# One attention and mixture-of-experts layer on one core: the four engines' work lists written out again in smaller pieces

## The chip, the cores and the metric

The kernel runs on one core of a Trainium2 chip. The metric is the device time of one execution in microseconds. In the text, PE is TensorE (matrix products and transposes), DVE is VectorE, ACT is ScalarE, POOL is GpSimd, and SP is SyncE, which only issues transfers. Every engine works through its own list of instructions in order; an instruction starts when the semaphores that stand before it in the list have reached their values.

## The reference

Input `x` has 4 batches of 512 tokens of 128 features. There are two halves, each with a residual:

```python
x = x + _layernorm(_L0_attn_ref(_layernorm(x), w_qkv, w_out))
x = x + _layernorm(_L0_ffn_ref(_layernorm(x), router_w, w1, w2, shared_gate_up, shared_down, shared_gate_w))
# attention: 16 heads of 8 features. The tokens are permuted in rows of a snake, cut in 4 segments of 128;
# each query of a segment attends to every second key of its segment (64 keys):
scores = jnp.einsum('bhsqd,bhskd->bhsqk', qh * scale, kd)
attn = jax.nn.softmax(scores, axis=-1)
# feed forward: 8 experts, the best 2 of each token with their softmax weights, and a shared expert
routed = jnp.einsum('ne,ned->nd', combine, einsum(silu(xf @ w1[e]), w2[e]))
shared = sigmoid(xf @ shared_gate_w) * (silu(gate) * up @ shared_down)
```

All values are float32. Every expert is computed for every token and weighted, with zero where it was not chosen.

## The kernel before

**Data.** A batch is 4 tiles of 128 tokens. All weights lie in SBUF. Products that need full precision are made of a high and a low part: `q_high`/`q_low` and `k_high`/`k_low` split the projections, `w1h`/`w1l` (made by ACT and by `w_low` on POOL, L268) the expert weights, `XH`/`XL` the feed-forward input.

**Attention of a batch b**, by the names of the steps:
- `normalise_x` (ACT), `x_T` (PE transposes), `x_copy` (ACT), `qkv` (PE; it becomes `q_project` and `k_project`), `qk_high` (ACT) and `qk_low` (DVE).
- `select_k` and `select_q` (PE) spread the features so that 16 heads lie in 4 groups; `k_rows` and `q_rows` (ACT, one group on DVE) copy them out. `k_blocks` (DVE, L1185, four instructions of 96x1024) writes the block-diagonal keys `Kb`, of which there are two buffers, by the parity of the batch.
- `scores_q(b, s)` (PE, L463) makes the scores of segment s with queries on the rows, in two halves of 8 heads, into two PSUM banks; `maxima` (DVE, L1208) takes the negated maximum of each half; `max_split` splits it in two parts, `max_T` (PE, L472) transposes them, `max_rows` (ACT and DVE) copies them under the queries `Qs`. They are so subtracted within the next product.
- `scores_k(b, s)` (PE, L486) makes the scores again with keys on the rows, in two halves; `exps` (ACT, L897); `attend` (PE, L503) multiplies by values and by ones; `attended` (ACT) copies, `attend_T` (PE, L516) transposes, `divide` (DVE, L1224 and L1226) normalises two segments at a time; `output_T` (PE, L522), `o_copy` (ACT), `project` (PE, L536), `y_copy` (ACT).
- `residual`, `residual2` (DVE) take the statistics of the projected rows, add the input, and take the statistics again. `powers` (POOL, L299) raises variances to -1/2; `neg_mean` (DVE, L1165) follows. `normalise_3` (ACT), `moe_in` (PE) and `x3_high`, `x3_low` bring the result in as the feed-forward input.

**Feed forward of a batch.** `router` (PE) gives the logits; `route` and `route2` (DVE) make the softmax, the two largest, and the weights `CW`, with the exponentials on ACT (batches 0 and 1) or POOL (`router_exp`, L284). `gate`, `up`, `expert_h` (PE, L355 to L357) are the first products, `shared_o`, `expert_o` (PE, L681) the second; `tanh`, `silu`, `silu_0`, `gated` the nonlinearity; `accumulate` (DVE) and `weight` (ACT) add the weighted outputs, `add_weighted` (POOL) sums those of ACT, `finish` and `finish_out` end a batch.

**Order.** It is written out by hand in each engine's block. A prologue does batch 0 up to its scores. A loop over i = 0, 1, 2 has scores and maxima of batch i + 1 beside exponentials and attention of batch i. Then a list without a loop has the attention of the last batch beside the experts of batch 0; this list ends at `gate(1)`. A last loop has the experts of batches 1 to 3. In the loop of DVE the order around a batch's end is `maxima(i + 1, 3)`, `max_split(i + 1)`, `k_blocks(i + 2)`, `divide(i, 1)`, `max_rows(i + 1)`. The dependent steps of `route2` on DVE are joined by `link`, which adds one to a common semaphore `step` and waits for it at once. Short `warm_up` products on PE fill waits of the prologue.

## Time and profile before

| | us |
|---|---|
| three runs | 180.89, 180.92, 183.22 |
| median | 180.92 |
| the profiled execution | 180.77 |
| its span, first to last instruction | 178.9 |

Busy in the span: PE 152.5, PE's weight loads 128.9 (beside its products), DVE 132.2, ACT 113.4, POOL 46.7. The mean granted clock of TensorE is 0.958 of full speed. The page's list of the chain that ended last puts 62% of the span to PE and 26% to DVE. The transfers are small: 6.01 MB, nearly all of it in the first 14 us.

A row of the timeline has start, duration, engine, line, operation, output and inputs, count, and in brackets the idle time of the engine before it with what ended it. A row of windows has the stretch, its length, busy time and count for PE, PE's weight loads, DVE, ACT and POOL, then the granted clock as a share of full speed, the share of the DMA engines, and GB/s.

### The profile page before, as it was taken

To read this page: it belongs to the slowest core of one execution; us is meant where nothing else is said; L and a number is where in the kernel's file an instruction comes from. 1 tells how busy PE (TensorE), PEld (TensorE's weight loads), DVE (VectorE), ACT (ScalarE), POOL (GpSimd) and SP (SyncE) were. 2 spreads that over 40 slices of the span, in tenths; PEclk is the share of its full clock that TensorE was granted. 3 is DMA by queue.
4 is the path that set the end of the run, shared out by engine and by line. 5 is a ranking of instruction groups with operands and counts; after the bars stand their busy time and mean duration, and the time that the engine had idled before them with its cause. 6 is when DMAs were issued, how large, how long until landed. Compare 5 with 4: busy or idle time off the path is not lost.

```text
span 178.9 us, 3632 instructions
## 1 busy us (share of the span) xinstructions
PE 152.5 (85%) x1188; PEld 128.9 (72%) x1188; DVE 132.2 (74%) x499; ACT 113.4 (63%) x269; POOL 46.7 (26%) x47
## 2 busy tenths in 40 slices
PE   6999797895499964999789999999999899969920
PEld 5787666673298642999578887979997899869920
DVE  7579889028955999328968876958999945896793
ACT  3787683834977565555496679944689376746803
POOL 5511003202001260002200220259552098202211
PEclk9999999889999999579999999999999999999995
DMA  5990630000000000000000000000000100100101
GB/s 170 314 330 12 146 94 2 4 0 0 0 0 4 0 4 0 0 0 0 5 2 0 4 0 4 0 0 2 4 0 2 59 4 0 57 4 0 52 11 59
DMA packets 10626, 6.01 MB, mean 34 GB/s; under 512 B 753, under 2 KB 10609, under 8 KB 10609
## 3 DMA queue, kind: packets, MB, share of 16 engines
q1 hardware_dynamic: 10192, 5.58, 11.1%
q10 hardware_dynamic: 416, 0.21, 0.4%
q8 instruction: 10, 0.16, 0.4%
q14 instruction: 8, 0.06, 0.1%
HBM read 3.69 MB, written 1.05 MB: 26 GB/s over the span
## 4 chain that ended last, share of the span: by engine, by line
PE 62%; DVE 26%; ACT 4%; issue 4%; POOL 1%; POOLq 0%; ACTq 0%; DVEq 0%
PE bank L681 15%; PE bank L486 7%; DVE negm L1208 6%; PE bank L355 5%; PE bank L356 4%; PE bank L357 4%; PE bank L352 4%; PE bank L463 3%; DVE Kb L1185 3%; PE bank L503 3%; PE bank L536 2%; DVE ST L1116 2%; DVE X L1364 2%; DVE Kb L1157 1%; PE bank L411 1%
## 5 line engine op out<-in xcount | busy, mean ns | idle before, releaser
L299 POOL TENSOR_TENSOR RS<-VE,nhalf 128x4 f32<-128x4 f32 x14 | 14.1, 1009 | 90.1 <-DVE VE L1124 90.1
L1208 DVE TENSOR_REDUCE negm<-bank 128x8 f32<-128x512 f32 x32 | 20.6, 684 | 13.9 <-PE bank L463 13.8
L1364 DVE SCALAR_TENSOR_TENSOR X<-bank,CW,X 128x128 f32<-128x128 f32 x80 | 22.5, 342 | 7.8 <-PE bank L681 7.7
L681 PEld LDWEIGHTS bank<-w2n,Pr 128*128 128x128 f32 x192 | 25.0, 191 | 2.0
L897 ACT ACTIVATE Pr<-bank 128x512 f32<-128x512 f32 x32 | 18.0, 598 | 12.4 <-PE bank L486 12.1
L681 PE MATMUL bank<-w2n,Pr 128*128 128x128 f32 x192 | 25.2, 275 | 0.0
L1019 ACT ACTIVATE Pr<-bank 128x512 f32<-128x512 f32 x27 | 16.3, 604 | 11.9 <-PE bank L357 11.8
L486 PE MATMUL bank<-Qs,Kb 128*128 128x128 f32 x128 | 19.7, 296 | 0.4 <-ACT Qs L837 0.2
L486 PEld LDWEIGHTS bank<-Qs,Kb 128*128 128x128 f32 x128 | 17.8, 208 | 2.0 <-issue 0.9
L355 PE MATMUL bank<-XH,w1h 128*128 128x512 f32 x32 | 15.2, 474 | 0.0
L315 POOL TENSOR_TENSOR Tm<-Tm 128x512 f32<-128x512 f32 x7 | 9.0, 1285 | 20.2 <-ACT Tm L1034 20.2
L1034 ACT ACTIVATE Tm<-bank,CW 128x128 f32<-128x128 f32 x44 | 12.5, 369 | 2.6 <-PE bank L681 2.6
L463 PE MATMUL bank<-Kb,Qs 96*128 96x256 f32 x64 | 13.2, 326 | 0.9 <-ACT Qs L863 0.5
L356 PE MATMUL bank<-XH,w1l 128*128 128x512 f32 x32 | 12.6, 394 | 0.0
L357 PE MATMUL bank<-XL,w1h 128*128 128x512 f32 x32 | 12.6, 393 | 0.0
L463 PEld LDWEIGHTS bank<-Kb,Qs 96*128 96x128 f32 x64 | 9.6, 206 | 4.1 <-issue 2.5
L284 POOL TENSOR_TENSOR EX<-base,DL 128x36 f32<-128x36 f32 x2 | 12.3, 6132 | 0.9 <-DVE DL L1257 0.9
L503 PE MATMUL bank<-Pr,Vb 128*32 128x128 f32 x256 | 10.7, 288 | 0.0
L352 PE MATMUL bank<-Y 128*128 128x256 f32 x24 | 8.9, 514 | 1.4 <-DVE Y L1288 1.4
L516 PE MATMUL bank<-cst,AVs 128*128 128x128 f32 x32 | 6.6, 287 | 3.2 <-DVE O L1226 1.6
L889 ACT ACTIVATE AVs<-bank 128x256 f32<-128x256 f32 x16 | 6.3, 395 | 4.4 <-PE bank L503 4.4
L681 PE MATMUL bank<-w2n,hs 128*128 128x128 f32 x64 | 8.7, 279 | 0.0
(158 smaller groups left out, 351.8 us busy)
## 6 DMA issues: line engine op xcount, KB each, us to landing
X<-in_L_attn_x SPq DMA_DIRECT2D x4, 256.0 KB, 4.0
Kb<-kone SPq DMA_DIRECT2D x8, 128.0 KB, 2.7
XP<-in_x_snake SPq DMA_DIRECT2D x3, 256.0 KB, 4.0
out<-XN SPq DMA_DIRECT2D x3, 256.0 KB, 2.2
w1n<-in_L_ffn_w SPq DMA_DIRECT2D x1, 512.0 KB, 4.8
w2n<-in_L_ffn_w SPq DMA_DIRECT2D x1, 512.0 KB, 5.9
out<-XN SPq DMA_DIRECT2D x2, 128.0 KB, 1.8
wqkv_n<-in_L_attn_w_qkv SPq DMA_DIRECT2D x1, 192.0 KB, 3.4
```

The lines of the kernel that those rows point to most:

```text
L352: mm(to[:, 0:width], Y[:, 0], Y[:].rearrange("p t d -> p (t d)")[:, 0:width], start=True, stop=True)
L355: mm(out_, wh, vh, start=True, stop=False)
L356: mm(out_, wl, vh, start=False, stop=False)
L357: return mm(out_, wh, vl, start=False, stop=True)
L463: i = mm(S1[n % 2][:, j * 256:(j + 1) * 256], Qs[0:MROW, b % 2, g, s * P:(s + 1) * P], Kb[0:MROW, b % 2, g, s], start=True, stop=True)
L486: i = mm(S2[s2_bank(n)][:, j * P:(j + 1) * P], Kb[:, b % 2, g, s, 2 * pr:2 * pr + 2], Qs[:, b % 2, g, s * P:(s + 1) * P], start=True, stop ...
L503: i = mm(PC[j * VW:(j + 1) * VW, (s % 2) * 2 * P + half * P:(s % 2) * 2 * P + (half + 1) * P], Vb[:, b % 2, s, half * 4 + j], Pr[:, n % 4, ...
L681: i = mm(ps[output_bank(n, s)][:, s * P:(s + 1) * P], lhs[:, s * P:(s + 1) * P], w, start=True, stop=True)
L897: A(Pr[:, n % 4], bank(S2[s2_bank(n)], 4), ACT.Exp).then_inc(S["ex"], 1)
L1019: A((hs0 if b == 0 else hs)[:, k % 3 if k >= 0 else 3], ps[hidden_bank(n)][:], ACT.Silu).then_inc(S["sh"], 1)
L1208: V.tensor_reduce(negm[:, b % 2, s, 8 * half:8 * half + 8], bank(S1[n % 2], 8, KEYS), AX.X, ALU.max, negate=True).then_inc(S["mx"], 1)
L1364: V.scalar_tensor_tensor(out=acc[:, b, t], in0=ps[output_bank(n)][:, t * P:(t + 1) * P], scalar=CW[:, b, t, k:k + 1], in1=acc[:, b, t], op ...
```

## The change

- The loops up to `gate(1)` are gone. Each engine's list up to there is written out step by step, in a new order, with the steps of attention, router and experts mixed more finely.
- `scores_q`, `scores_k`, `maxima`, `exps` and ACT's `max_rows` are called for one half at a time in many places; `normalise_x` and `normalise_3` for single tiles. `qkv`, `qk_high`, `qk_low`, `residual` and `residual2` are cut in their parts (`q_project`, `k_project`, `q_high`, `k_high`, `q_low`, `k_low`, `spread_y`, `gather`, `add_rows`, `spread_r`). `select_k` can be called by halves.
- `link` and its semaphore `step` are gone. `route` and `route2` are cut in ten steps; two of them have a new semaphore (`iv`, `eqs`), and the sum counts on `sm`, which is now waited for at 2 per batch.
- The waits of PE for the weights of the experts stand at their first use. ACT fills the ones for the keys (`key_ones`) before its first normalisation. The two preparations of low parts on POOL stand elsewhere in its list.
- The last loop, batches 1 to 3, keeps its order; only the parts have their new names.

The core of the diff. The list of ACT, the lists of PE after batch 1 and of DVE after `max_split(2)` are left out; they alternate in the same manner.

```diff
@@ gpsimd
-            powers_0(0)
-            powers_0(1)
-            powers(0, 1)
-            key_columns(0)
-            key_columns(1)
-            powers(0, 2)
-            w_low(rwl[:], rwn[:], rwh[:], S["rwhs"], 1, S["rwls"])
-            w_low(gul[:], gun[:], guh[:], S["guhs"], 1, S["guls"])
...
+            powers_0(0)
+            powers_0(1)
+            powers(0, 1)
+            powers(0, 2)
+            powers(0, 3)
+            key_columns(0)
+            key_columns(1)
+            key_columns(2)
+            powers(1, 0)
+            experts_low()
+            powers(2, 0)
+            router_low()
+            key_columns(3)
+            powers(1, 1)
+            shared_low()
+            powers(2, 1)
+            powers(1, 2)
+            powers(2, 2)
+            add_weighted(0)
+            router_exp(2)
+            powers(1, 3)
+            powers(3, 0)
+            powers(2, 3)
+            add_weighted(1)
+            powers(3, 1)
+            router_exp(3)
+            add_weighted(2)
+            powers(3, 2)
+            add_weighted(3)
...
@@ tensor, from the end of batch 0's scores to those of batch 2
+            select_q(1, 3)
+            x_T(2)
+            max_T(0)
+            values(1)
+            k_project(2)
+            scores_k(0, 0)
+            q_project(2)
+            scores_q(1, 0, (0,))
+            scores_k(0, 1, (0,))
+            scores_q(1, 0, (1,))
+            scores_k(0, 1, (1,))
+            attend(0, 0)
+            scores_k(0, 2, (0,))
+            scores_q(1, 1)
+            attend(0, 1)
+            scores_k(0, 2, (1,))
+            scores_q(1, 2, (0,))
+            scores_k(0, 3, (0,))
+            scores_q(1, 2, (1,))
+            attend_T(0, 0)
+            attend_T(0, 1)
+            attend(0, 2)
+            scores_q(1, 3, (0,))
+            scores_k(0, 3, (1,))
+            scores_q(1, 3, (1,))
+            select_k(2, (0,))
+            attend(0, 3)
+            attend_T(0, 2)
+            select_k(2, (1,))
+            attend_T(0, 3)
+            max_T(1)
+            select_q(2, 0)
+            select_q(2, 1)
+            output_T(0)
+            select_q(2, 2)
+            select_q(2, 3)
+            scores_k(1, 0)
+            project(0)
+            scores_q(2, 0, (0,))
...
@@ scalar, start
+            key_ones()
+            normalise_x_0(0)
+            x_copy_0(0)
+            normalise_x_0(1)
+            k_high_0(0)
+            q_high_0(0)
...
@@ vector, steps of the router
-            def route2(b):
...
-                link(V.tensor_reduce(nmx[:, b, 1], EX[:, b, :, 0:E], AX.X, ALU.add))
-                dve.wait_ge(S["sm"], b + 1)
+                V.tensor_reduce(nmx[:, b, 1], EX[:, b, :, 0:E], AX.X, ALU.add).then_inc(S["sm"], 1)
...
+            def router_inverse(b):
+
+                dve.wait_ge(S["sm"], 2 * (b + 1))
                 V.reciprocal(SG[:, b], EZ[:, b]).then_inc(S["sg"], 1)
-                link(V.reciprocal(nmx[:, b, 2], nmx[:, b, 1]))
+                V.reciprocal(nmx[:, b, 2], nmx[:, b, 1]).then_inc(S["iv"], 1)
...
@@ vector, from the end of batch 0's maxima
+            maxima(0, 3)
+            max_split(0)
+            q_rows(1)
+            k_blocks(1, (1,))
+            max_rows(0)
+            k_blocks(1, (2, 3))
+            maxima(1, 0, (0,))
+            neg_mean(0, 3)
+            k_low(2)
+            maxima(1, 0, (1,))
+            q_low(2)
+            maxima(1, 1)
+            maxima(1, 2)
+            divide(0, 0)
+            maxima(1, 3)
+            max_split(1)
+            divide(0, 1)
+            k_blocks(2, (0,))
+            max_rows(1)
+            k_blocks(2, (1, 2, 3))
+            q_rows(2)
+            maxima(2, 0, (0,))
+            spread_y(0)
+            gather(1, 0)
+            maxima(2, 0, (1,))
+            maxima(2, 1, (0,))
+            neg_mean(1, 0)
+            maxima(2, 1, (1,))
+            add_rows(0)
+            maxima(2, 2, (0,))
+            spread_r(0)
+            maxima(2, 2, (1,))
+            k_low(3)
+            maxima(2, 3, (0,))
+            q_low(3)
+            maxima(2, 3, (1,))
+            divide(1, 0)
+            gather(2, 0)
+            max_split(2)
...
```

## Rows read from the trace of the kernel before

**Rows 1.** The page: busy time by engine, and the granted clock in 40 slices.
```profile
PE 152.5 (85%) x1188; PEld 128.9 (72%) x1188; DVE 132.2 (74%) x499; ACT 113.4 (63%) x269; POOL 46.7 (26%) x47
...
PEclk9999999889999999579999999999999999999995
```

**Rows 2.** Windows cut at the four `max_T` and at `gate(1)`; columns as told above.
```profile
0.00:22.67 22.67, 19.60 (x109) 15.92 (x109) 16.83 (x50) 14.94 (x34) 6.50 (x18) 1.00 0.69 194
22.67:45.74 23.07, 19.03 (x160) 13.91 (x159) 14.10 (x41) 13.63 (x31) 3.54 (x5) 0.93 0.07 17
45.74:67.43 21.69, 17.13 (x169) 13.79 (x169) 17.31 (x47) 15.59 (x34) 4.96 (x4) 1.00 0.01 2
67.43:90.55 23.12, 19.00 (x166) 16.25 (x167) 16.07 (x50) 12.13 (x26) 2.02 (x2) 0.85 0.01 1
90.55:119.37 28.82, 28.24 (x250) 24.25 (x251) 21.31 (x102) 22.55 (x55) 4.57 (x4) 1.00 0.01 1
119.37:178.90 59.53, 49.51 (x341) 44.74 (x339) 46.53 (x214) 34.59 (x93) 25.17 (x14) 0.96 0.06 19
```

**Rows 3.** Timeline of PE: the first matmul and six waits.
```profile
1.45 5.46 PE L352 MATMUL bank<-Y 128*128 128x256 f32 x12 [1.45 <-DVE Y L1288]
...
20.82 0.33 PE L424 MATMUL bank<-kch,sel 128*96 128x256 f32 x1 [0.90 <-DVE kcl L1177]
...
31.74 1.39 PE L405 MATMUL bank<-cst,XN 128*128 128x128 f32 x4 [0.97 <-ACT XN L822]
...
41.53 0.33 PE L424 MATMUL bank<-kch,sel 128*96 128x256 f32 x1 [0.88 <-DVE kcl L1177]
...
49.05 0.66 PE L522 MATMUL bank<-cst,O 128*128 128x128 f32 x4 [2.26 <-DVE O L1226]
...
63.31 0.33 PE L424 MATMUL bank<-kch,sel 128*96 128x256 f32 x1 [1.04 <-DVE kcl L1177]
...
70.81 0.66 PE L522 MATMUL bank<-cst,O 128*128 128x128 f32 x4 [2.26 <-DVE O L1226]
```

**Rows 4.** Timeline of DVE before the first output transposes.
```profile
45.54 2.73 DVE L1185 TENSOR_SCALAR Kb<-Ks,cst 96x1024 fp32r<-96x1024 f32 x4
...
48.57 0.42 DVE L1226 TENSOR_TENSOR O<-bank,rden 128x256 f32<-128x256 f32 x1
```

**Rows 5.** Windows around the two stretches of lower clock.
```profile
34.00:38.00 4.00, 4.00 (x27) 2.54 (x25) 1.29 (x2) 1.30 (x3) 0.66 (x1) 0.57 0.02 4
71.00:79.00 8.00, 8.00 (x52) 7.45 (x51) 2.44 (x4) 3.75 (x7) 0.00 (x0) 0.57 0.00 0
```

**Rows 6.** Timeline of POOL and DVE: the low part of the expert weights.
```profile
63.29 2.38 POOL L268 TENSOR_TENSOR w1l<-w1n,w1h 128x1024 fp32r<-128x1024 f32 x1
...
63.80 1.89 DVE L1165 SCALAR_TENSOR_TENSOR NM<-MV,RS 128x4 f32<-128x4 f32 x1
```

**Rows 7.** Timeline of ACT: first normalisation, and the ones for the keys.
```profile
5.49 0.86 ACT L785 ACTIVATE XN<-XP,NM,RS 128x128 f32<-128x128 f32 x2
...
16.63 1.05 ACT L939 ACTIVATE kone<-cst 32x1024 fp32r<-32x1024 f32 x1
```

**Rows 8.** Timeline of PE: `scores_k` whole, then by halves, with the next instruction.
```profile
56.06 1.09 PE L486 MATMUL bank<-Qs,Kb 128*128 128x128 f32 x8
56.99 0.40 PE L516 MATMUL bank<-cst,AVs 128*128 128x128 f32 x2
...
97.47 0.63 PE L486 MATMUL bank<-Qs,Kb 128*128 128x128 f32 x4
97.94 0.44 PE L355 MATMUL bank<-XH,w1h 128*128 128x512 f32 x1
```

**Rows 9.** Timelines: a power on POOL, and the longest wait at a `link`.
```profile
29.87 1.01 POOL L299 TENSOR_TENSOR RS<-VE,nhalf 128x4 f32<-128x4 f32 x1 [13.03 <-DVE VE L1124]
...
153.28 0.18 DVE L1267 RECIPROCAL SG<-EZ 128x4 f32<-128x4 f32 x1 [0.37 <-DVE nmx L1265]
```

**Rows 10.** Timeline of PE: the one long wait of the last stage.
```profile
157.99 1.16 PE L681 MATMUL bank<-dwn,Pr 128*128 128x128 f32 x8 [1.46 <-DVE Pr L1421]
```

More of the change, by code:

```diff
@@ new lines, in _ @@
+            warm_up(1, TH)
+            x_T_0(0)
+            qkv_0(0)
+            warm_up(1, TH)
+            x_T_0(1)
+            select_k_0(0)
+            qkv_0(1)
+            select_q_0(0, 0)
+            select_q_0(0, 1)
+            warm_up(1, TH)
+            x_T(1)
+            scores_q(0, 0, (0,))
+            select_k_0(1)
+            scores_q(0, 0, (1,))
+            k_project(1)
+            select_q_0(1, 0)
+            select_q_0(1, 1)
+            q_project(1)
+            scores_q(0, 1, (0,))
@@ new lines, in _ @@
+            scores_k(1, 1, (0,))
+            scores_q(2, 0, (1,))
+            scores_q(2, 1, (0,))
+            scores_k(1, 1, (1,))
+            values(2)
+            x_T(3)
+            scores_q(2, 1, (1,))
+            scores_k(1, 2, (0,))
+            scores_q(2, 2, (0,))
+            scores_k(1, 2, (1,))
+            attend(1, 1)
+            scores_q(2, 2, (1,))
+            scores_k(1, 3, (0,))
+            k_project(3)
+            attend_T(1, 0)
+            q_project(3)
+            attend_T(1, 1)
@@ new lines, in _ @@
+            scores_q(2, 3, (0,))
+            scores_k(1, 3, (1,))
+            scores_q(2, 3, (1,))
+            attend(1, 2)
+            select_k(3)
+            attend(1, 3)
+            select_q(3, 0)
+            attend_T(1, 2)
+            select_q(3, 1)
+            attend_T(1, 3)
+            max_T(2)
+            select_q(3, 2)
+            select_q(3, 3)
+            output_T(1)
+            scores_k(2, 0)
+            project(1)
+            scores_k(2, 1)
+            scores_q(3, 0, (0,))
@@ L751, in _ @@
             expert_o(0, 6)
+            output_T(3)
             gate(1)
@@ new lines, in _ @@
+            gather(0, 2)
+            neg_mean(0, 1)
+            k_low_0(0)
+            spread_x(3)
+            q_low_0(0)
+            gather(0, 3)
+            k_blocks_0(0, (0, 1, 2, 3))
+            k_low_0(1)
+            q_low_0(1)
+            neg_mean(0, 2)
+            maxima(0, 0)
+            k_blocks_0(1, (0,))
+            k_low(1)
+            k_blocks_0(1, (1, 2, 3))
+            maxima(0, 1, (0,))
+            q_low(1)
+            maxima(0, 1, (1,))
+            maxima(0, 2)
@@ new lines, in _ @@
+            divide(1, 0)
+            gather(2, 0)
+            max_split(2)
+            k_blocks(3, (0,))
+            divide(1, 1)
+            neg_mean(2, 0)
+            max_rows(2)
+            k_blocks(3, (1, 2, 3))
+            q_rows(3)
+            spread_y(1)
+            maxima(3, 0)
+            gather(1, 1)
+            maxima(3, 1)
+            x3_low(0)
+            neg_mean(1, 1)
+            maxima(3, 2)
+            add_rows(1)
+            divide(2, 0)
+            maxima(3, 3, (0,))
@@ L1427, in _ @@
+            logits(0)
+            maxima(3, 3, (1,))
+            max_split(3)
+            divide(2, 1)
             silu_0(-1)
-            x3_low(i - 2)
+            max_rows(3)
+            largest_logit(0)
+            below_largest(0)
             gated(0)
-            route2(i - 3)
-            residual(i - 1)
+            spread_r(1)
+            gather(2, 1)
+            spread_y(2)
+            gather(1, 2)
             silu_0(0)
-            residual2(i - 1)
+            neg_mean(2, 1)
```

662 lines of the change are left out of this document (332 added, 330 removed), and 2 rows, old and new, of the table names.

## The prediction, made before the changed kernel ran

> **What bounds the kernel now.** I read the page first. TensorE is busy 85% of the span, and the line of the granted clock has two dips [rows 1]. Then I cut the span at the transposes of the row maxima (`max_T`), which stand once in every batch, and at `gate(1)`, the first gated product of the second batch [rows 2]. The sixth stage, 59.53 us, has its list of work untouched. The change is in the five stages before it, 119.37 us. There PE is idle 3.07, 4.04, 4.56, 4.12 and 0.58 us (length of each stage less its busy time). The fifth stage, where attention of the last batch and the experts of the first already alternate, is full: that part of the order is interleaved today. The three attention stages are not.
>
> The timeline of PE tells why [rows 3]. In each stage it stops at the same places: before `select_k` for the low part of the keys (0.90, 0.88, 1.04), before a transpose of x for `normalise_x` (0.97), and twice for 2.26 at `output_T`. The 2.26 is an order, not work: DVE does four key blocks (2.73 us) before `divide`, although the output transposes wait for the divide and the blocks are wanted only later [rows 4]. Behind these holes the clock is granted at half, 1.2 instead of 2.4 GHz, in two stretches: mean 0.57 over 4 us and 0.57 over 8 us [rows 5]. PE is busy all through both, so they cost 0.43 x 4 + 0.43 x 8 = 5.2 us. The reader should see that the idle share of PE understates the loss: 16.4 us of holes and 5.2 us of slow work.
>
> **What can be had at most.** Of the 3.07 us in the first stage 1.45 is the wait for the first memset and stays (first matmul at 1.45 [rows 3]). The rest: 1.62 + 4.04 + 4.56 + 4.12 + 0.58 = 14.9, and with the clock 20.1 us. The profiled execution took 180.77 us (span 178.9, 1.9 around it), within 0.2 of the median 180.92. So the floor, with PE never idle before `gate(1)`, is 160.7.
>
> **The change, part by part.** *The same instructions.* Matmuls, copies, maxima and exponentials keep their number and shape; nothing is loaded twice. Halving a pair costs PE nothing: `scores_k` in one piece of eight takes 56.99 - 56.06 = 0.93 us to the next instruction, in pieces of four 97.94 - 97.47 = 0.47 each, twice 0.47 = 0.94 [rows 8]. I take 0; the bound above is 0.1 us for each of some 25 new splits, 2.5 us, were each wait to show.
>
> *Stages 2 to 4.* I walked the new lists of PE, ACT and DVE side by side from `max_T(0)`, each step as long as in the trace, each starting at the latest of its waits. The projections of the next batch but one (`x_T(2)`, `k_project(2)`, `q_project(2)`) and all of `select_q(1)` now stand before or around `scores_k(0, 0)`; `k_low(2)` and `q_low(2)` are done some 6 us before `select_k(2)` asks for them, so the wait of 0.9 to 1.0 goes. `divide(0, 1)` stands ahead of `k_blocks(2)`, so `output_T(0)` finds its rows at once: 2.26 goes, twice. What is late next is the key blocks. `scores_q(2, 0)` waits for all four, which end about 5 us after `max_split(1)` (0.8 divide + 2.7 blocks + 0.7 `max_rows`, and the wait for the last transpose); PE meanwhile has `max_T`, four `select_q`, `output_T`, `scores_k(1, 0)` and `project(0)`, 4.6 us by the same rows. Cover and wait are within half a microsecond; without this cover it would be a hole of up to 5.
>
> The three stages hold 55.16 us of busy PE [rows 2], 50.0 without the slow clock. DVE has 47.5 in them, 1.7 of it a collision (below). So once PE's holes are closed DVE is busy over nine tenths of the time, in order, and some of its work waits for the same PE. PE can't be kept full throughout.
>
> *The collision.* GpSimd computes `w1l` for 2.38 us, and a negated mean on DVE that is usually 0.16 lasts 1.89 beside it, to the same end [rows 6]. Today that falls where DVE has spare time later. In the new order `experts_low` is queued straight behind `powers(1, 0)`, and `neg_mean(1, 0)` stands on DVE between maxima that `scores_q(2, 2)` needs. I charge the whole 1.7 us; the bound below is 0.
>
> *The start.* ACT fills the ones (1.05 us) before the first `normalise_x_0`, which now starts at 5.49; today it does so later, at 16.6 [rows 7]. Everything to the first maxima hangs on that row: +1.0. The eight transfers of these ones are issued by SP behind its loads, so they go out earlier and aren't wanted before `scores_k(0, 0)`: 0. On GpSimd `key_columns(0)` is moved behind two more powers of 1.01 us [rows 9], which wait for `spread_x(3)`; by the walk it is ready at about 13 us and `values(0)` asks at about 17: 0, else up to 1.
>
> *Stage 5.* `gate(0)` is drawn ahead of it and the work is otherwise the same; I expect it as full as now and take none of its 0.58. ACT has the waits on `silu` and `attended(3, 3)` later in its list, PE has moved the last attention to match.
>
> *Router steps that signal singly.* Five waits of the old chain on DVE become waits of their own semaphores. Where steps follow each other nothing changes; the longest wait that one shows is 0.37 [rows 9]. In stage 5 other work now lies between. At most 1 us, taken as 0.
>
> *The last stage.* Same lists, and its one hole, 1.46 at `shared_o(3)` [rows 10], is made inside it: 0.
>
> **Sum.** 20.1 at most; less 0.6 (stage 5 not improved), less 1.0 (start), less 1.7 (collision), less 2.2 for waits that I don't see: 3% of the remaining 72 us, against the 2% (0.58 of 28.82) that the best stage loses with DVE at 74%. Gain 14.6: 180.8 - 14.6 = 166.2, so **166 us**. The walk itself, without the last term, ends `gate(1)` near 101, some 18 us earlier.
>
> **The rivals.**
> *DVE becomes the bound of stages 2 to 4.* For it: 47.5 us of DVE against 50.0 of PE. Against it: the walk finds a DVE list with slack of 0.3 to 1 us at most maxima. DVE is now idle 8.97 + 4.38 + 7.05 = 20.4 us in them; if only half of that goes, the stages shrink by 10.2: 180.8 - 10.2 = 170.6, about **171**. 0.19.
> *The clock.* Today both slow stretches follow stages with holes [rows 3, 5]. The new order trades few long holes for many short ones and for transposes between them. The five stages hold 103.0 us of busy PE [rows 2], 97.8 without the slow clock. If all of it ran at the mean of today's worst stage, 0.85, these 98 us would take 115 and with 1.5 us at the head and 2 of waits end near 119, which is today's 119.4: **181**, no change. For *slower* (over 184.5) the front must pass 123, so a mean clock under 98/119.5 = 0.82 over all of it. Against: stage 5, the most finely mixed one, has 1.00. 0.04 for no change, 0.03 for slower.
> The Trainium skill, in "TensorE: Matmul & The Clock Gate", section "A second HAM failure mode: psum-queue depth-cycling", says that short idles between groups of matmuls, as buffers are cycled, make the clock swing between its two levels. By that rule this change would do what the clock rival says, near 181; the rows of stage 5 do not agree with it, those of stages 2 and 4 do not exclude it.
> *Waits close completely.* No collision, no residue: 161 to 163. 0.12.
> *The change does nothing because the chain of dependences is the limit.* The last maximum of a batch leads to its split, transposes, rows, scores, exponentials, attention, output; but the maxima of the next batch don't wait for that chain, only for the key buffer two batches back. So this could hold a part only; 179 or more, 0.02.
>
> **Chances and range.** The forecast, 163 to 169: 0.60; with full closing 0.12, DVE as the bound 0.19, clock 0.07, nothing gained 0.02. The range takes in full closing and the DVE case: **161 to 172**. A difference of over 2% (3.6 us) is what a measurement can tell: faster 0.91, same 0.06, slower 0.03.
>
> **What would show it.** `max_T(1)`, `max_T(2)` and `max_T(3)` near 38, 56 and 72 us (today 45.74, 67.43, 90.55), and `gate(1)` between 102 and 106; no wait of `output_T` over 1 us; no `select_k` waiting for `kcl`; granted clock 1.00 in the third to fifth stage; DVE busy over 85% from `max_T(1)` to `max_T(3)`; the last stage 59.5 within 0.5. Wrong would be: a first maximum later than 14.5 us; a long wait of `scores_q(2, 0)` or `scores_q(3, 0)` for key blocks; a half clock over more than 6 us; or a last stage longer than now because the weights of the later routers come late.

## The result, and the profile after

| | before | after |
|---|---|---|
| median, us | 180.90 | 159.58 |
| all runs of this comparison | 178.85 to 183.22 (4) | 159.45 to 159.74 (4) |
| ratio, 95% interval | | 0.8855 (0.8782 to 0.8929) |
| profiled execution, its span | 180.77, 178.9 | 159.69, 157.6 |

The kernel is faster by 21.3 us. The forecast was 166, with a range of 161 to 172: the direction is right, and the time lies 1.4 us under the range. Executions of one kernel can differ by some per cent, with a lower mean clock in the longer ones; the ratios leave out executions more than 1.5% above the fastest of their kernel.

The page of the kernel after: busy time by engine, the granted clock in 40 slices, and the shares of the chain that ended last.

```profile
PE 144.3 (92%) x1188; PEld 125.1 (79%) x1188; DVE 132.3 (84%) x499; ACT 113.8 (72%) x269; POOL 47.0 (30%) x47
...
PEclk9999999999999999999999999999999999999996
...
PE 77%; DVE 9%; ACT 5%; issue 3%; DMA 2%; POOLq 1%; ACTq 1%; POOL 0%; DVEq 0%
```

Beside [rows 1]: the same 1188 matmuls and 499 instructions of DVE, with DVE busy for the same 132 us, but PE's busy time has *fallen* by 8.2 us, and the two dips of the clock in the list are gone (the last slice is low in both). In the chain PE has gone from 62% to 77%, DVE from 26% to 9%.

Windows of the kernel after, cut at the same instructions as [rows 2]: the four `max_T`, then `gate(1)`.

```profile
0.00:23.63 23.63, 20.68 (x120) 17.29 (x121) 20.22 (x70) 17.64 (x40) 8.53 (x20) 1.00 0.75 202
23.63:37.07 13.44, 13.44 (x147) 10.96 (x146) 10.95 (x20) 11.14 (x24) 0.91 (x1) 1.00 0.00 1
37.07:56.00 18.93, 18.11 (x175) 14.57 (x173) 18.05 (x46) 15.19 (x32) 4.30 (x3) 1.00 0.00 1
56.00:71.71 15.71, 15.71 (x169) 13.72 (x168) 13.81 (x36) 11.70 (x26) 2.55 (x5) 1.00 0.01 3
71.71:98.58 26.87, 26.85 (x250) 23.86 (x248) 21.98 (x112) 22.82 (x56) 5.27 (x5) 1.00 0.01 2
98.58:157.60 59.02, 49.48 (x341) 44.72 (x339) 47.26 (x217) 35.26 (x94) 25.45 (x15) 0.98 0.07 19
```

The second and the fourth stage have no idle PE at all. From the first to the last `max_T` DVE is busy 10.95 + 18.05 + 13.81 = 42.8 of 48.08 us (89%), and all five stages have full clock. The stages don't hold quite the same work as before (work of later batches was moved forward into the first), so only the sum of the five can be compared: 119.37 us then, 98.58 now.

Five waits of PE are all that the waits view shows in those five stages. Here are the four longest in PE's timeline:

```profile
1.45 4.89 PE L363 MATMUL bank<-Y 128*128 128x256 f32 x14 [1.45 <-DVE Y L1538]
...
7.03 0.62 PE L376 MATMUL bank<-cst,XN 128*128 128x128 f32 x2 [0.69 <-ACT XN L864]
...
8.12 0.50 PE L385 MATMUL bank<-xT,wqkv_n 128*128 128x128 f32 x2 [0.47 <-ACT xT L870]
...
48.76 0.48 PE L479 MATMUL bank<-Kb,Qs 96*128 96x256 f32 x2 [0.82 <-DVE negm L1350]
```

The fifth is 0.3 us for `Qs` in the first stage. `select_k` waits for nothing any more, and neither does `output_T`, which had 2.26 twice [rows 3]. The timeline of DVE shows why: the divide stands directly ahead of the key blocks, where it stood behind four of them [rows 4].

```profile
37.27 0.36 DVE L1366 RECIPROCAL rden<-bank 128x32 f32<-128x32 f32 x1 [0.92 <-PE bank L532]
37.66 0.42 DVE L1368 TENSOR_TENSOR O<-bank,rden 128x256 f32<-128x256 f32 x1
38.00 0.74 DVE L1326 TENSOR_SCALAR Kb<-Ks,cst 96x1024 fp32r<-96x1024 f32 x1
```

**Where the 21.1 us of the profiled executions came from.** Idle time of PE ahead of `gate(1)`: 16.37 before, now 2.95 + 0 + 0.82 + 0 + 0.02 = 3.79, so 12.58. Clock: 5.2, both half-speed stretches, as the prediction worked them out. The last stage: 59.53 - 59.02 = 0.5. Time around the span: 1.87 before, 2.09 now, so -0.2. That makes 18.0. The remaining 3.05 are time in which PE *counted as busy* before, at full clock: 103.0 - 5.2 = 97.8 us in the five stages, against 94.8 now. I had taken this 97.8 as fixed work.

### The profile page after: what moved, and what is told of

Its sections match the earlier page's. It is cut to its first block, busy times and chain, and to the rows that moved or that the text cites. A ratio compares the mean times of both kernels' runs of the same rounds, so it can differ in the third digit from the quotient of the medians.

```text
span 157.6 us, 3642 instructions
## 1 busy us (share of the span) xinstructions
PE 144.3 (92%) x1188; PEld 125.1 (79%) x1188; DVE 132.3 (84%) x499; ACT 113.8 (72%) x269; POOL 47.0 (30%) x47
## 3 DMA queue, kind: packets, MB, share of 16 engines
HBM read 3.69 MB, written 1.05 MB: 30 GB/s over the span
## 4 chain that ended last, share of the span: by engine, by line
PE 77%; DVE 9%; ACT 5%; issue 3%; DMA 2%; POOLq 1%; ACTq 1%; POOL 0%; DVEq 0%
PE bank L625 18%; PE bank L502 8%; PE bank L366 6%; PE bank L479 5%; PE bank L519 5%; PE bank L367 5%; PE bank L368 5%; PE bank L552 3%; PE bank L532 3%; DMA cst<-in_consts 2%; PE bank L451 2%; DVE X L1477 2%; PE bank L459 2%; PE bank L452 2%; PE bank L423 2%
## 5 line engine op out<-in xcount | busy, mean ns | idle before, releaser
L1350 DVE TENSOR_REDUCE negm<-bank 128x8 f32<-128x512 f32 x32 | 21.4, 685 | 3.0 <-PE bank L479 2.6
L1045 ACT ACTIVATE Pr<-bank 128x512 f32<-128x512 f32 x27 | 16.3, 605 | 8.9 <-PE bank L368 8.7
L980 ACT ACTIVATE Pr<-bank 128x512 f32<-128x512 f32 x32 | 18.7, 597 | 4.0 <-PE bank L502 3.6
L502 PE MATMUL bank<-Qs,Kb 128*128 128x128 f32 x128 | 18.8, 274 | 0.0
L502 PEld LDWEIGHTS bank<-Qs,Kb 128*128 128x128 f32 x128 | 16.8, 191 | 2.1 <-issue 1.2
L479 PE MATMUL bank<-Kb,Qs 96*128 96x256 f32 x64 | 14.2, 314 | 1.2 <-DVE negm L1350 0.8
L363 PE MATMUL bank<-Y 128*128 128x256 f32 x24 | 7.7, 463 | 1.4 <-DVE Y L1538 1.4
L1070 ACT ACTIVATE XN<-X,mh 128x128 f32<-128x128 f32 x16 | 5.2, 407 | 5.2 <-DVE mh L1516 5.2
L1326 DVE TENSOR_SCALAR Kb<-Ks,cst 96x1024 fp32r<-96x1024 f32 x12 | 8.8, 767 | 0.1
```

The lines of the kernel that those rows point to most:

```text
L479: i = mm(S1[n % 2][:, j * 256:(j + 1) * 256], Qs[0:MROW, b % 2, g, s * P:(s + 1) * P], Kb[0:MROW, b % 2, g, s], start=True, stop=True)
L502: i = mm(S2[s2_bank(n)][:, j * P:(j + 1) * P], Kb[:, b % 2, g, s, 2 * pr:2 * pr + 2], Qs[:, b % 2, g, s * P:(s + 1) * P], start=True, stop ...
L980: A(Pr[:, n % 4], bank(S2[s2_bank(n)], 4), ACT.Exp).then_inc(S["ex"], 1)
L1045: A((hs0 if b == 0 else hs)[:, k % 3 if k >= 0 else 3], ps[hidden_bank(n)][:], ACT.Silu).then_inc(S["sh"], 1)
L1350: V.tensor_reduce(negm[:, b % 2, s, 8 * half:8 * half + 8], bank(S1[n % 2], 8, KEYS), AX.X, ALU.max, negate=True).then_inc(S["mx"], 1)
```

## The experiments

Each is an edit of the kernel before or of the kernel after, the two kernels of the case. Medians are of four or five executions, and the rows are from one of them. The kernel after ran again only beside the next three; the later runs are set against the same 159.6 us. Differences under 1 us are therefore read from the stages, and not from the first one: it took from 23.5 to 24.4 us in seven traces whose start is the same.

**The kernel after once more, as the base of the next three.**

> The changed kernel itself, as the base line on the same chip as the next three. 159.5 to 159.7 us, span 157.6; max_T(1) at 37.1, max_T(2) at 56.0, gate(1) at 98.6.

159.62 us (159.43 to 161.24). The kernel repeats, with one execution of four 1.6 us longer.

**The ones for the keys, back to a later place on ACT.**

```
-            key_ones()
             normalise_x_0(0)
             ...
             q_rows_0(1, 1)
+            key_ones()
             normalise_x(2, (3,))
```

> The changed kernel with key_ones moved back on ACT, from before the first normalisation to behind q_rows_0(1, 1). Theory (the start hangs on the first normalisation, so the 1.05 us of the ones is paid in full): the first transposes of x move from 7.03 to about 6.1 us and the end comes 0.8 to 1.0 us earlier, 158.7. Rival (ACT is full up to 24 us, so the same 1.05 us is paid later in its list): under 0.3 us, 159.4.

159.96 us (159.88 to 160.37): no gain, 0.3 longer. Timelines of this kernel, PE (the first product on copied rows, then `select_q`) and ACT:

```profile
7.46 0.50 PE L385 MATMUL bank<-xT,wqkv_n 128*128 128x128 f32 x2 [0.47 <-ACT xT L870]
...
20.84 0.48 PE L451 MATMUL bank<-qch,sel 128*96 128x512 f32 x1 [0.66 <-ACT Ks L951]
...
18.63 1.05 ACT L996 ACTIVATE kone<-cst 32x1024 fp32r<-32x1024 f32 x1
```

The first product came 0.66 us earlier, as the theory said, and PE then lost the same time at 20.84, since ACT has no spare time in the first stage. This is the rival: nothing is gained by moving the ones within ACT's list. (The 0.3 us is within what the first stage varies by.)

**`experts_low` ahead of `powers(1, 0)` on POOL**, so that it doesn't run beside `neg_mean(1, 0)`.

```
             key_columns(2)
+            experts_low()
             powers(1, 0)
-            experts_low()
             powers(2, 0)
```

> The changed kernel with experts_low on GpSimd ahead of powers(1, 0), where GpSimd idles. Theory (the collision costs what was charged in the prediction): neg_mean(1, 0) falls from 2.33 to about 0.16 us, the 0.82 us wait of scores_q(2, 2) goes, stage 3 (max_T(1) to max_T(2)) shrinks from 18.9 to about 18.0: 158.7 us. Rival (DVE is the bound of stage 3 anyway, or the collision only meets another instruction): stage 3 within 0.3 of 18.9, 159.5 us.

In the kernel after, the timelines of POOL and DVE show the collision again, longer than in [rows 6], and its end is what the 0.82 us wait of PE at 48.76 goes back to:

```profile
45.62 2.37 POOL L268 TENSOR_TENSOR w1l<-w1n,w1h 128x1024 fp32r<-128x1024 f32 x1
...
45.68 2.33 DVE L1296 SCALAR_TENSOR_TENSOR NM<-MV,RS 128x4 f32<-128x4 f32 x1
```

With the edit the same negated mean takes 0.17, and the third stage 18.08 instead of 18.93, with PE busy all through (timeline of DVE, then the window of the third stage):

```profile
46.44 0.17 DVE L1296 SCALAR_TENSOR_TENSOR NM<-MV,RS 128x4 f32<-128x4 f32 x1
...
37.82:55.90 18.08, 18.08 (x174) 14.56 (x173) 16.06 (x46) 15.13 (x32) 2.12 (x3) 1.00 0.00 1
```

Total 159.37 (158.95 to 159.78), less than the spread can tell. In the profiled execution (159.63 us) the first stage, which the edit doesn't touch, was 24.39 us long instead of 23.63, and so hid the gain. The stage settles it: the collision costs PE 0.85 us, not the 2.2 that DVE loses.

**Both divides back behind four key blocks**, as in the old order; nothing else.

```
             max_split(1)
+            k_blocks(2, (0, 1, 2, 3))
             divide(0, 1)
-            k_blocks(2, (0,))
             max_rows(1)
-            k_blocks(2, (1, 2, 3))
             ...
             max_split(2)
-            k_blocks(3, (0,))
+            k_blocks(3, (0, 1, 2, 3))
             divide(1, 1)
             neg_mean(2, 0)
             max_rows(2)
-            k_blocks(3, (1, 2, 3))
```

> The changed kernel with divide(0, 1) and divide(1, 1) put back behind all four key blocks. Theory (the order at the end of a batch is what removed the two waits of 2.26 us): output_T(0) and output_T(1) wait 2 to 3 us each and the clock dips again behind them; 164 to 167 us. Rival (it is the finer mixing that covers, and the place of divide matters little): each wait under 1 us and 160 to 161 us.

165.47 us (165.34 to 166.05), 5.9 longer. Timeline of PE at the two output transposes, and the window of the third stage:

```profile
41.51 0.93 PE L538 MATMUL bank<-cst,O 128*128 128x128 f32 x4 [2.60 <-DVE O L1368]
...
63.40 0.66 PE L538 MATMUL bank<-cst,O 128*128 128x128 f32 x4 [1.60 <-DVE O L1368]
...
37.38:60.27 22.89, 19.35 (x175) 15.88 (x174) 18.16 (x47) 15.41 (x32) 4.31 (x3) 0.93 0.00 1
```

Both holes come back, 4.2 us, and behind the 2.60 the clock is granted at half for a while: the stage's mean is 0.93, and its busy PE is 19.35 instead of 18.11. In the new order, this one edit is worth 5.9 us.

**All split pairs made whole again**, 46 calls of `scores_q`, `scores_k`, `maxima` and `exps`, at the place of the second half.

```
-            scores_q(1, 0, (0,))
-            scores_k(0, 1, (0,))
-            scores_q(1, 0, (1,))
-            scores_k(0, 1, (1,))
+            scores_q(1, 0)
+            scores_k(0, 1)
             ...
```

> The changed kernel with all 46 split calls of scores_q, scores_k, maxima and exps made whole again, each pair at the place of its second half; the rest of the order is kept. Theory (what fills PE is the order of the steps; the halves are a fine tuning): 160.5 to 163 us, with new waits of 0.3 to 0.8 us of PE for an exponential or a maximum. Rival (the small pieces are what keeps PE full): several waits over 1 us in each batch and a clock dip, 166 us or more.

167.12 us (165.28 to 170.54), ratio to the kernel before 0.9253 (0.9166 to 0.9341). It looks as though small pieces were worth 7.5 us everywhere, but the stages say otherwise. The rows are from the longest execution, of 170.54 us. Its third and fourth stage, from `max_T(1)` to `max_T(3)`, take 35.30 us together, against 34.64; the second takes 13.41, against 13.44, and the first 23.98. All the rest is in the fifth. Its window, and two of its four waits in PE's timeline:

```profile
72.69:109.43 36.74, 33.52 (x249) 29.17 (x248) 22.06 (x112) 23.34 (x56) 5.25 (x5) 0.81 0.00 1
...
77.55 0.63 PE L502 MATMUL bank<-Qs,Kb 128*128 128x128 f32 x4 [0.87 <-ACT Pr L954]
...
95.90 1.09 PE L502 MATMUL bank<-Qs,Kb 128*128 128x128 f32 x4 [0.78 <-ACT Pr L954]
```

In that stage `scores_k` of the last batch has a single PSUM bank for its two halves, so a whole pair waits for the exponential of its first half. It was in halves there before the change too. How much of the loss is clock differs between executions: this one had a mean clock of 0.945, while the one of 165.28 us had 0.990, as high as the kernel after, and was still 5.7 us longer than it. So the waits cost several us by themselves, and a half clock like the 0.81 of this stage comes on top only in some executions.

**Only the 33 pairs of the middle whole**, with the last batch's `scores_k` and `exps` and batch 0's `scores_q` and `maxima` left in halves.

> The changed kernel with the split calls made whole in stages 2 to 4 only (33 pairs); the last batch's scores_k and exps, whose scores have a single bank and which were split before the change too, stay in halves. Theory (small pieces matter only where one bank must be emptied before it is filled again, and the order does the rest): stages 2 to 4 longer by 0.5 to 1.0 us in sum as in the run with whole pairs everywhere (35.3 against 34.6 us), stage 5 as in the changed kernel at 26.9 us; 160.2 to 160.8 us. Rival (the small pieces keep the middle full when the start shifts): 162 us or more.

160.24 us (160.15 to 160.47), 0.7 longer than the kernel after. From `max_T(1)` to `max_T(3)` it takes 35.32 us, against 34.64, and the fifth stage 26.88, against 26.87. The window of the third stage, where more than half of the 0.7 lies:

```profile
36.93:56.26 19.33, 18.35 (x175) 14.66 (x174) 18.04 (x46) 15.07 (x32) 4.19 (x3) 1.00 0.00 1
```

So the small pieces, the most conspicuous part of the change, are worth 0.7 us in the middle stages. The halves of batch 0 in the first stage are also new and stay in this run; with them whole too, the first stage above was 23.98 us, within what it varies by. What the change gained there came from the order.

**The router's waits right behind their steps**, as `link` had them.

```
                 dve.wait_ge(S["ez"], 2 * (b + 1))
                 V.tensor_reduce(nmx[:, b, 1], EX[:, b, :, 0:E], AX.X, ALU.add).then_inc(S["sm"], 1)
+                dve.wait_ge(S["sm"], 2 * (b + 1))
```

(and the same behind the reciprocals, on `iv`, and behind `combine`, on `eqs`.)

> The changed kernel with DVE waiting at once behind the sum, the reciprocal and the combination of the router, as link did. Theory (single signals are worth nothing by themselves, since the order keeps other work between only in the first two batches): 159.6 to 159.9 us. Rival (the chained waits cost a few tenths each in all four batches): 160.5 us or more.

159.94 us (159.78 to 160.22), 0.3 longer. It lies in the last stage, 59.30 us against 59.02; the fifth is the same (26.86). Single signalling of the router's steps is worth 0.3 us, close to the nothing of the prediction.

**The other way round: the one edit of the divide, in the kernel before.**

```
                 max_split(i + 1)
+                divide(i, 1)
                 if p1:
                     k_blocks(i + 2)
-                divide(i, 1)
```

> The kernel before with one edit: divide(i, 1) ahead of k_blocks(i + 2) on DVE. Theory (the two waits of 2.26 us are made by this order alone and the half clock behind the second of them comes from it): both waits under 0.5 us, no half clock near 71 to 79 us, the key blocks 0.8 us later; 173 to 175 us. Rival (the wait moves to scores_q behind the key blocks, and the clock dips all the same): 178 to 181 us.

178.03 us (177.91 to 178.12); the kernel before in the same comparison 180.36, ratio 0.9894 (0.9829 to 0.9958). Both waits of 2.26 are gone, and yet it gains 2.3 us where the same order, undone in the kernel after, cost 5.9. Timeline of PE behind the former hole, then the window of the third stage, which was 21.69 at clock 1.00 [rows 2]:

```profile
47.95 0.47 PE L435 MATMUL bank<-qch,sel 128*96 128x512 f32 x1 [0.72 <-ACT Qs L863]
...
49.67 0.47 PE L435 MATMUL bank<-qch,sel 128*96 128x512 f32 x1 [1.02 <-ACT Qs L863]
...
45.72:68.78 23.06, 19.01 (x169) 15.41 (x169) 17.32 (x47) 15.81 (x34) 4.96 (x4) 0.93 0.01 1
```

PE now arrives earlier at `select_q`, which waits for ACT's `q_rows`, so that the idle time of the third stage falls only from 4.56 to 4.05 us. The slow clock has moved: the third stage, which had none behind its wait of 2.26, has some now behind waits of 0.72 and 1.02, while the fourth is at 1.00 and 19.02 us long (it was 23.12 at 0.85). My theory of 173 to 175 was wrong here; the rival of 178 to 181, that the wait goes to the next late thing, was right.

**Products without use in the hole before `output_T`, in the kernel before**, to keep PE active there without moving any work. First eight of them, then five.

```
                 if i >= 1:
+                    warm_up(8, TH)
                     output_T(i - 1)
```

> The kernel before with eight extra products of 128x256 ahead of output_T(0) and output_T(1), in the waits of 2.26 us, to a bank that is free there; they add work and no result. Theory (the hole before 70.8 us is what makes the clock fall behind it): no half clock at 71 to 79 us, 3 to 3.5 us less, 177.5 us. Rival (the clock falls for another reason, as it did not fall behind the first hole of the same length): the dip stays and the time is 180.5 to 181.5 us.

> The kernel before with five extra products of 128x256 instead of eight in its two waits of 2.26 us: eight took 3.45 us each time, more than the wait; five take 2.15. Theory (the long half-clock stretch of stage 4 is caused by the hole before it): stage 3 as before at 21.7 us, stage 4 shorter by 2 to 3.4 us, 177.5 to 179 us. Rival (dips come back elsewhere, the clock is not governed by this hole): 180.5 to 181.5 us and the same total of half-clock time, about 10 us.

Eight: 180.94 us (178.94 to 181.02), ratio 1.0029 (0.9949 to 1.0109), no difference that can be told; the products took longer than the hole (timeline of PE: 3.61 us where the hole had been 2.26). Five: 178.90 (175.91 to 180.06), against 179.04 of the kernel before beside it; the ratio of 0.987 (0.9754 to 0.9986) leaves out its two longer executions, and the result is unclear. The windows of the fourth stage, first with eight, then with five:

```profile
66.34:87.24 20.90, 19.03 (x182) 16.38 (x183) 16.05 (x50) 11.58 (x26) 2.02 (x2) 0.98 0.00 2
```

```profile
68.08:88.09 20.01, 17.95 (x176) 15.15 (x177) 16.11 (x51) 11.66 (x26) 2.02 (x2) 1.00 0.01 2
```

This stage was 23.12 at 0.85 [rows 2]. With five products in the hole its half clock is gone and it is 3.1 us shorter, the five products included, although no real work of the stage was moved. But the half clock has only gone elsewhere. The clock line of the page with five products, and the window of its second stage, which was 23.07 at 0.93:

```profile
PEclk9999999789799999999879999999999999999995
...
22.36:46.37 24.01, 19.98 (x160) 14.63 (x159) 15.05 (x42) 14.23 (x32) 3.53 (x5) 0.87 0.06 15
```

The fifth stage, which was 28.82 at 1.00, is 30.39 at 0.95 (with eight products 30.11 at 0.95). Summed over the stages as length times the missing share of the clock, the half clock costs 5.1 us in this execution, as it did before. This is what the rival said: dips come back elsewhere, and their sum stays. So neither this nor the edit of the divide shows that the hole of 2.26 causes the half clock behind it. The four executions with five products had mean clocks of 0.958, 0.959, 0.976 and 0.987, and the executions of the kernel before had 0.938 to 0.987 without any edit.

What all sixteen traces of this case do show is coarser. In eight of them PE idles less than 1.0 us in each of the stages two to five (the kernel after, twice, and six variants of it), and all of these stages have a clock of 1.00. In the other eight at least one of these stages has more idle time, and at least one of them, not always that one, is below 1.00.

**The projections of batch 2 and the values of batch 1 back to where the old order had them**, beside the second and third segment, with their copies on ACT and DVE.

```
-            x_T(2)
             ...
-            values(1)
-            k_project(2)
             ...
-            q_project(2)
             ...
             attend(0, 1)
             ...
+            values(1)
+            x_T(2)
             ...
+            q_project(2)
+            k_project(2)
```

> The changed kernel with values(1), x_T(2) and the projections of batch 2 (and their copies and low parts on ACT and DVE) put back to where the kernel before had them, beside the second and third segment. Theory (this early work is what covers max_rows(0) and takes away the waits of select_k(2)): PE waits about 1 us before scores_k(0, 0) and about 1 us before select_k(2), stage 2 longer by 2 to 3 us, or 4 to 5 with a clock dip behind; 161.6 to 164 us. Rival (the finer mixing finds other cover): 160.2 us or less.

162.03 us (161.74 to 164.95), 2.4 longer. Timeline of PE, in the longest execution, of 164.95 us:

```profile
25.23 1.11 PE L502 MATMUL bank<-Qs,Kb 128*128 128x128 f32 x8 [1.16 <-ACT Qs L916]
...
27.15 0.48 PE L479 MATMUL bank<-Kb,Qs 96*128 96x256 f32 x2 [0.81 <-issue]
```

Without the projections in front of it, the first `scores_k` finds the rows of maxima not yet copied. That half of the theory holds. The other half doesn't: the wait of `select_k(2)` for `kcl` did not come back. In its place stands the 0.81, for which the profile shows no releaser. The two waits together, 1.97 us, are nearly the 2.4 of the median. The second stage of this execution has a clock of 0.82, but the four shorter ones had mean clocks of 0.985 to 0.987 over the whole kernel, within the 0.980 to 0.993 of the kernel after: the same holes brought a long half clock in one execution of five.

**Both of these at once**: divides late and projections late.

> The changed kernel with both orders put back: the late projections of batch 2 and divide behind the key blocks. Theory (the prices of the holes add, since each stops PE at another place): the sum of the two separate losses over the changed kernel within 1 us (divide alone cost 5.9 us), so 168 to 170 us. Rival (one hole gives the other its cover): less than 1 us above the run with divide alone, under 166.5 us.

170.73 us (169.29 to 176.16), 11.1 longer, where the two alone add to 5.9 + 2.4 = 8.3. That is neither the sum within 1 us nor the rival. The windows of the second and the fourth stage in the longest execution, of 176.16 us:

```profile
23.28:43.57 20.29, 18.34 (x149) 15.38 (x149) 10.90 (x20) 11.22 (x24) 0.65 (x1) 0.75 0.00 1
...
66.14:88.17 22.03, 20.41 (x169) 17.78 (x168) 14.20 (x36) 12.15 (x26) 3.54 (x5) 0.77 0.01 2
```

The second stage has the same 149 products as with late projections alone, and the fourth the 169 of the kernel after, where PE was busy for 15.71. The holes add up: PE idles 7.1 us in the stages two to four, against 0.8 in the kernel after. That is 6.3 of the 11.1 us. The rest goes with the clock: the execution of the median, 170.73 us, had a mean of 0.956, and the 0.75 and 0.77 of the rows are those of the longest one, at 0.919. The order also brings back the scatter between executions that the kernel before has and the kernel after hasn't.

**In the last loop, `gated(b + 1)` ahead of `accumulate(b, 6)` for b = 2.** The long wait of the last stage is still there in the kernel after; it is at `shared_o(3)`, for `gated(3)`, which DVE had behind an accumulation.

```
                     expert_weights(B - 1)
+                if b == 2:
+                    gated(b + 1)
                 accumulate(b, 6)
                 ...
-                if b + 1 < B:
+                if b + 1 < B and b != 2:
                     gated(b + 1)
```

> The changed kernel with one edit in the last stage: on DVE gated(3) stands ahead of accumulate(2, 6). The hole of 1.46 us before shared_o(3) waits for gated(3), which stands behind the router weights of batch 3 and that accumulation (1.04 us). Theory: the wait falls to 0.4 us and the end comes 1.0 us earlier, 158.5 us. Rival (DVE is without a gap there, so the delayed accumulation is waited for next): 159.3 us or more.

158.50 us (158.40 to 158.78), 1.1 less. Timeline of PE, where the wait was 1.46:

```profile
135.69 1.16 PE L625 MATMUL bank<-dwn,Pr 128*128 128x128 f32 x8 [0.41 <-DVE Pr L1534]
```

**Three edits together:** this one, `experts_low` early, and the ones for the keys filled by POOL instead of ACT, between `powers(0, 2)` and `powers(0, 3)`.

```
             powers(0, 2)
+            key_ones()
             powers(0, 3)
             ...
-            key_ones()
             normalise_x_0(0)
```

> The changed kernel with three edits: the ones for the keys are filled by GpSimd between its early powers instead of by ACT ahead of the first normalisation; experts_low ahead of powers(1, 0); gated(3) ahead of accumulate(2, 6). Theory: the ones leave ACT's full list, so that the 0.7 us of an earlier start is kept, the collision gives 0.8, gated 1.0: 157.0 us, with a first transpose of x near 6.4 us. Rival (the start is set by the landing of x and what is won there is waited for before max_T(0)): 157.8 us.

157.28 us (156.84 to 157.47), ratio to the kernel before 0.8767 (0.8700 to 0.8834). It beats both kernels, by 2.3 us the one after. Timeline of POOL, and PE's first product on copied rows:

```profile
9.94 1.04 POOL L305 CAST kone<-cst 32x1024 fp32r<-32x1024 f32 x1
...
7.12 0.50 PE L395 MATMUL bank<-xT,wqkv_n 128*128 128x128 f32 x2 [0.47 <-ACT xT L880]
```

This product starts 1.0 us earlier, and the first stage is 23.11 long instead of 23.63. The edit that failed on ACT works on POOL, which has the time. The parts add up: 0.5 here, 0.85 for the collision, 1.1 for `gated(3)`, for 2.3 in the median; the 0.5 is the least certain of them, as a stage length of one execution.

## Why the prediction was right in direction and too small

**What held.** The holes at `output_T` and `select_k` went. The old divide order costs 5.9 us in the new list, its two holes and the slow clock behind them; the prediction had 2 x 2.26 for the holes and 5.2 for all of the clock. The clock was 1.00 in all five stages. `max_T(1)` to `max_T(3)` came at 37.07, 56.00 and 71.71, for 38, 56 and 72, and the first maximum at 13.77, under 14.5. DVE was busy (18.05 + 13.81) / (18.93 + 15.71) = 92% from `max_T(1)` to `max_T(3)`, for "over 85%". `scores_q(2, 0)` never waited for key blocks. The last stage was 59.02, inside 59.5 with 0.5. The router's signals were worth 0.3 at most.

**What failed: "the floor, with PE never idle before `gate(1)`, is 160.7".** The profiled execution took 159.69, with 3.79 us of idle time left in PE. A floor made from PE's busy time is no floor. This is the step that put the measured time outside the range: with every charge at zero the sum still ended at 160.7, and 161 was the lower bound for that reason. The prediction held the 97.8 us of busy PE ahead of `gate(1)` (103.0 less 5.2 for the clock) for fixed work; the same products took 94.8.

Of these 3.05 us, about 1.2 are in the warm-up products of the start: L352 held 8.9 us in the five stages, the same line, now L363, 7.7. This part is chance and gains nothing. In the sixteen traces these 24 records took from 7.6 to 9.1 us; in the trace of `gated(3)`, whose first stage has the same list, they took 8.7, PE was busy for 21.38 instead of 20.68, and the stage was just as long (23.65 against 23.63). What they lose in busy time comes back as idle time ahead of the first transposes. The remaining 1.85 are spread out. The clearest place is the fifth stage, at full clock both times. Groups of instructions of that stage, PE, before and then after; the columns are count, busy us, mean ns of one, and idle time before them:

```profile
L681 PE MATMUL bank<-w2n,hs 128*128 128x128 f32 x56 | 7.7, 280 | 0.0
L486 PE MATMUL bank<-Qs,Kb 128*128 128x128 f32 x32 | 5.1, 282 | 0.1
```

```profile
L625 PE MATMUL bank<-w2n,hs 128*128 128x128 f32 x56 | 7.1, 276 | 0.0
L502 PE MATMUL bank<-Qs,Kb 128*128 128x128 f32 x32 | 4.9, 276 | 0.0
```

The same 56 and 32 products took 7.7 + 5.1 = 12.8 us of busy time and now take 12.0. The profile models the ends of matmuls, which overlap the next one's start ([rows 8]: a product of 1.09 us, and the next instruction starts after 0.93). A wait shorter than this overlap is not counted as idle: it looks like a slightly longer product. Fewer such waits is my reading of the 1.85 us; no run isolates it, so this cause stays open.

The Trainium skill, in "Perfetto Trace Analysis", section "Identifying the Most-Contended Engine", says that the busy share of matmuls is not a good measure of how close TensorE is to its limit, since they are pipelined, and that the operations done against the peak and the busy share of the weight loads are to be used instead. By the second of these PE stood at 72% before [rows 1], not 85%, and is at 79% now. The trace agrees in so far as there was more room than the busy time of 152.5 us showed. I had read the 128.9 us of weight loads and not used them.

**What failed: "less 2.2 for waits that I don't see: 3% of the remaining 72 us".** It was an allowance and not a row, and no row gives the 72 either. In the second and fourth stage the idle time of PE is 0.00, in the fifth 0.02. Where every wait lies behind other work, nothing is left over. The fifth stage, where I took no gain, gave 0.56 of idle time and part of the busy time above.

**Sizes.** The collision was charged 1.7. DVE lost even more (2.33 against 0.17), but PE only 0.82, since `scores_q` had some slack there. The start was charged 1.0, for ACT's first row moving from 5.49 [rows 7] to 6.39. It did move by 0.9, but the first maximum by 0.33 only (13.44 to 13.77), and with the ones on POOL the first stage is 0.5 shorter. Term by term, in idle time of PE: the fifth stage was charged 0.6 and kept 0.02; the collision 1.7 and 0.82; the start 1.0 and 1.50 (2.95 less the 1.45 of the first wait; with the slower warm-up of the `gated(3)` trace 0.82); the unseen waits 2.2 and 0. So 5.5 were charged and 2.3 found, which is 3.2 of the error; the busy time is 3.05, the last stage and the time around the span 0.3. Together they are the 6.5 us between the gain forecast (14.6) and that of the profiled execution (21.1).

`gate(1)` came at 98.58, for "102 to 106"; the walk's own end of 101 was nearer. The sum does not match the walk: without the 2.2 its charges put `gate(1)` at 119.4 - 16.8 = 102.6, so they were 1.6 us above what the walk had found, and the allowance took the forecast further off.

**The rivals.** "Waits close completely, 161 to 163" was the nearest, given 0.12, and its own bound was short by the false floor. DVE as the bound didn't happen at 92% busy: what counts is that the maxima are ready when PE frees a bank, and only the one maximum behind the collision was late. The clock rival fell completely.

The Trainium skill's rule on psum-queue depth-cycling ("TensorE: Matmul & The Clock Gate"), that many short idles between groups make the clock swing, would have given the 181 of the clock rival. This trace does not agree for this kernel: the interleaved order has clock 1.00 in five stages. The half clock came behind the 2.60 of the divide experiment (0.93 in that stage), and in the longest execution with late projections in the stage with the 1.16 and 0.81 (0.82). It did not come behind the single 0.82 at 48.76 in the kernel after, nor in the third stage of the kernel before, with its 2.26 (1.00). What comes nearest to the rule is the fifth stage with whole pairs: four waits of 0.78 to 0.87, each at the hand-over of one PSUM bank, in 36.74 us, and a mean clock of 0.81, though another execution of that kernel had 0.990 over its whole length. So such waits can matter when they repeat; the change makes none of them.

**What stays open.** Two orders, divide and projections, are worth 11.1 of the 21 us when they are undone in the new list. The other 10 I put down to the many waits of 0.5 to 1.0 us (`select_k` for `kcl`, transposes of x and of attention) with the clock beside them; no run takes them apart. Which hole is followed by a half clock, and in which execution, stays open too. The numbers of the divide in both kernels (2.3 and 5.9) say that such a list has no fixed price for each item.

## What to carry to other kernels

A hole in the engine that bounds the kernel is closed only when the next late thing is also moved: one edit gave 2.3 us in an otherwise unchanged list, and the same edit undone in a finished list cost 5.9. Put first what the other engine waits for (divide before key blocks), and place ready work (projections) ahead of a product that needs a fresh copy; in this kernel cutting instructions smaller mattered mainly where a single buffer is shared (7.5 us over all pairs, 0.7 without those of the single bank). Don't build a floor from the busy time of matmuls, and don't add a percentage for waits that the walk hasn't found.

## What the runs showed of the hardware

- The clock raises the price of holes. Two edits cost 5.9 and 2.4 us alone and 11.1 together, 6.3 of it idle time; the mean clock of the median execution with both was 0.956, against 0.980 to 0.993 in the executions of the kernel after.
- The clock differs between executions of one kernel. The kernel before had means of 0.938 to 0.987 and took 175.8 to 184.3 us over all its runs in these comparisons; the kernel after, with few holes, 159.4 to 161.2.
- With one hole of 2.26 us filled there was no half clock behind it in the one trace taken (20.01 at 1.00, where it had been 23.12 at 0.85), but in the same execution it came in the second stage (0.87) and in the fifth (0.95), for the same 5.1 us in sum.
- Some elementwise instructions of POOL hold up an instruction of DVE with two inputs in SBUF until they end. Beside `w1l` (128x1024, 2.37 us) the 128x4 negated mean took 2.33 us, and 0.17 alone. In the kernel after, at 97.89 us, a 128x32 sum (`EQ`, L1454) took 1.05 beside POOL's 128x512 sum `Tm`, and 0.19 elsewhere. Beside the same `w1l` in the kernel before, `divide`, with one input in PSUM, took its usual 0.43, and at 100.07 us in the kernel after a 128x32 product of two SBUF inputs took 0.18 beside POOL's exponentials for the router (6.14 us), so not every one of POOL's instructions does it.
- The warm-up products at the very start are slow while the recorded clock is 1.00: the first 12 records took 5.46 us, 0.46 each [rows 3]; two of the same shape, later, 0.59 with 0.43 us to the next instruction, 0.21 each. Their pace differs between executions: the same first 14 took 4.89 us in the kernel after and 5.88 with `gated(3)` moved.
